# An attention and int8 feed-forward layer on one core: TensorE's order by pairs of slots, and q and k projected into one bank

## The reference

```python
qkv = encodings @ attn_w.T + attn_b                      # 16 heads of 8
mask = jnp.arange(n)[:, None] <= jnp.arange(n)[None, :]
scores = jnp.einsum('bhki,bhqi->bhkq', k, q) / math.sqrt(HEAD)
probs = jax.nn.softmax(jnp.where(mask, scores, NEG_INF), axis=2)
combined = jnp.einsum('bhkq,bhkl->bhql', probs, v)
attn = combined.transpose(0, 2, 1, 3).reshape(b, n, HIDDEN) @ out_w.T + out_b
x = _layernorm(x + attn)
q_lhs = round(x / lhs_scale); q_rhs = round(rhs / rhs_scale)  # int8, absmax scales
x = _layernorm(x + (q_lhs @ q_rhs) * lhs_scale * rhs_scale)
```

## Time and profile before

| | |
|---|---|
| three runs | 284.0, 283.8, 280.09 us; median 283.8 |
| profiled execution | 284.06 us, span 282.3 us, mean granted clock 0.952 |
| PE busy | 244.5 us (87%) |
| DVE busy | 195.1 us (69%) |
| ACT busy | 188.1 us (67%) |
| POOL busy | 121.8 us (43%) |

### The profile page before, as it was taken

One profiled execution on the slowest core, in us unless ns is written; L12 is line 12 of the kernel. 1 busy time (PEld: TensorE's weight loads), 2 busy tenths in 40 slices (PEclk: granted clock), 3 DMA queues, 4 the chain that ended last, 5 costly groups with the idle time before them and its releaser, 6 DMA issues.

```text
span 282.3 us, 8298 instructions
## 1 busy us (share of the span) xinstructions
PE 244.5 (87%) x3075; PEld 171.2 (61%) x3077; DVE 195.1 (69%) x545; ACT 188.1 (67%) x434; POOL 121.8 (43%) x236
## 2 busy tenths in 40 slices
PE   4179747999999999999999999999999999999420
PEld 2037525676767676767676767676767677565200
DVE  7927853576869696868686868686868797624331
ACT  4202033677687787878787878787878777798341
POOL 7930840041525454545453535353535141532542
PEclk9999985999999999999999999999999999999855
DMA  3385777337554765476547654757466410110001
GB/s 93 111 189 121 165 154 196 77 116 152 173 93 134 133 193 92 151 134 192 91 153 135 192 91 151 135 170 118 151 116 190 76 41 15 31 37 16 7 19 37
DMA packets 50887, 32.77 MB, mean 116 GB/s; under 512 B 7200, under 2 KB 50848, under 8 KB 50848
## 3 DMA queue, kind: packets, MB, share of 16 engines
q1 hardware_dynamic: 50848, 32.26, 47.2%
HBM read 17.17 MB, written 14.68 MB: 113 GB/s over the span
## 4 chain that ended last, share of the span: by engine, by line
PE 81%; DVE 7%; issue 4%; POOL 3%; ACT 3%; DMA 1%; ACTq 0%; SPq 0%; POOLq 0%; DVEq 0%
PE pv_bank L860 18%; PE dve_bank L823 17%; PE act_bank L823 13%; PE act_bank L881 6%; PE dve_bank L826 5%; PE act_bank L826 5%; PE act_bank L891 3%; PE dve_bank L905 3%; PE dve_bank L923 3%; PE pv_bank L960 3%; PE act_bank L914 1%; PE dve_bank L871 1%; PE dve_bank L942 1%; PE act_bank L933 1%; POOL rstd L444 1%
## 5 line engine op out<-in xcount | busy, mean ns | idle before, releaser
L642 DVE TRANSPOSE_TENSOR_REDUCE part_max<-dve_bank 128x16 f32<-128x512 f32 (+1 forms) x192 | 115.8, 615 | 42.7 <-PE dve_bank L826 40.6
L481 ACT ACTIVATE probs<-act_bank 128x512 f32<-128x512 f32 (+1 forms) x192 | 101.2, 530 | 38.0 <-PE act_bank L826 37.1
L823 PE MATMUL act_bank<-q_move,k_stat 128*128 128x128 bf16 (+3 forms) x512 | 68.2, 236 | 6.2 <-issue 6.2
L823 PE MATMUL dve_bank<-q_move,k_stat 124*128 124x128 bf16 (+3 forms) x512 | 71.1, 241 | 1.6 <-DMA k_stat<-imagek 1.3
L860 PE MATMUL pv_bank<-probs,v_stat 128*32 128x256 f32 (+3 forms) x1024 | 61.1, 311 | 0.0
L823 PEld LDWEIGHTS dve_bank<-q_move,k_stat 124*128 124x128 bf16 x512 | 40.3, 117 | 28.9 <-DVE part_max L642 7.5
L419 POOL TENSOR_TENSOR qk_rest<-qk_f,qk_parts 128x512 f32<-128x512 f32 x15 | 17.4, 1162 | 75.5 <-ACT qk_f L499 72.4
L823 PEld LDWEIGHTS act_bank<-q_move,k_stat 128*128 128x128 bf16 x512 | 42.0, 114 | 10.7 <-issue 8.2
L826 PE MATMUL dve_bank<-causal,identb 128*128 128x128 bf16 (+1 forms) x192 | 46.5, 242 | 0.0
L826 PE MATMUL act_bank<-causal,identb 128*128 128x128 bf16 (+1 forms) x192 | 46.0, 240 | 0.0
L498 ACT ACTIVATE qk_parts<-act_bank,bias 128x256 bf16<-128x256 f32 x32 | 21.0, 655 | 26.6 <-PE act_bank L881 24.6
(11 more groups left out here) (87 smaller groups left out, 319.1 us busy)
## 6 DMA issues: line engine op xcount, KB each, us to landing
imageq<-qk_parts SPq DMA_DIRECT2D x32, 192.0 KB, 2.1
imagek<-qk_parts SPq DMA_DIRECT2D x32, 192.0 KB, 2.1
q_move<-imageq SPq DMA_DIRECT2D x32, 192.0 KB, 3.7
k_stat<-imagek SPq DMA_DIRECT2D x32, 192.0 KB, 4.4
xt_in<-xt_dram SPq DMA_DIRECT2D x16, 128.0 KB, 4.6
x_in<-x_dram SPq DMA_DIRECT2D x16, 128.0 KB, 2.4
out_dram<-o SPq DMA_DIRECT2D x16, 128.0 KB, 2.0
q_move<-shift SPq DMA_DIRECT2D x32, 8.0 KB
```

The lines of the kernel that those rows point to most:

```text
L481: act.activation(probs[u][:, 0:cols], act_bank[at % ACT_BANKS][:, 0:cols], ACT.Exp, scale=SCALE).then_inc(act_emptied, 1)
L642: dve.tensor_reduce(o32, dve_bank[at % DVE_BANKS][:, 0:n * (TOK - key)].rearrange("k (c q) -> k c q", q=32), op=ALU.max, axis=AX.X, apply_ ...
L823: pe.matmul(tiles[:, j, :], keys, q_move[b % QK_RING][0:rows, p0 + j, key:TOK], start=(j == 0), stop=False, skip_group_check=True)
```

## The change

It replaces the order within a phase. The score units stay where they are, but the other work of TensorE goes only behind odd slots, so that four score units (two for the maximum, two for the exponential) stand together. The value groups are six pairs of units where they were eight groups. q and k of a batch go into the two halves of one `act_bank`; ACT still empties q behind one slot's exponential and k behind the next one's, and only k's last activation says that the bank is empty. Because ACT then empties uses in another order than they were filled, two more tables (`ACT_DONE`, `ACT_FREE`) say what TensorE has to wait for. ACT and DVE have their extras moved to fit: `pv_from_psum` from slot 3 to 4, `norm1` to 5, q to 7 and k to 8, `heads_d` to 9, `round_z` to 10, `norm2` behind the last `zq`; on DVE `scale_ffn` to 3, the shift and both steps of `normalise` to 5.

```diff
-PV_GROUPS = [(0, 1), (2, 3), (4,), (5,), (6, 7), (8, 9), (10,), (11,)]
+PV_GROUPS = [(u, u + 1) for u in range(0, NU, 2)]
...
-ACT_EXTRAS = {1: [("v", 1)], 6: [("q", 4)], 7: [("k", 4)], 8: [("heads", -1)], 11: [("zq", -2)]}
-DVE_EXTRAS = {2: [("ffn", -3)], 4: [("shift", 1)], 5: [("pv", -1)], 11: [("out", -1)]}
+ACT_EXTRAS = {1: [("v", 1)], 7: [("qk", 4)], 9: [("heads", -1)], 11: [("zq", -2)]}
+ACT_EMPTIED = {1: [("v", 1)], 8: [("qk", 4)], 9: [("heads", -1)], 11: [("zq", -2)]}
+DVE_EXTRAS = {3: [("ffn", -3)], 5: [("shift", 1), ("pv", -1)], 11: [("out", -1)]}
...
+ACT_DONE = ring_places(lambda b, u: ("exp", b, u), ACT_EMPTIED)
+ACT_FREE = [max(ACT_DONE[name] for name in list(ACT_AT)[:n + 1]) for n in range(len(ACT_AT))]
...
@@ qk_from_psum
-                act.wait_ge(act_filled, at + 1)
-                src = act_bank[at % ACT_BANKS][:, 0:TOK]
+                    act.wait_ge(act_filled, at + 1)
+                src = act_bank[at % ACT_BANKS][:, w * TOK:(w + 1) * TOK]
...
-                act.activation(whole, src, ACT.Identity, bias=bias[:, w:w + 1]).then_inc(act_emptied, 1)
+                last = act.activation(whole, src, ACT.Identity, bias=bias[:, w:w + 1])
+                if w == 1:
+                    last.then_inc(act_emptied, 1)
...
@@ ScalarE's phase
-                    if u == 3:
+                    if u == 4:
                         pv_from_psum(b - 1)
...
@@ act_ring
-                    pe.wait_ge(act_emptied, at + 1 - ACT_BANKS)
+                    pe.wait_ge(act_emptied, ACT_FREE[at - ACT_BANKS] + 1)
...
@@ project_qk
+                for w in range(2):
+                    last = pe.matmul(bank[:, w * TOK:(w + 1) * TOK], wqkv[:, w, :], xt_in[b % XT_RING][:, :],
+                                     start=(w == 0), stop=True, skip_group_check=True)
+                last.then_inc(act_filled, 1)
...
@@ TensorE's phase, as it is after
+                    if u == 1:
+                        pv(b - 1, 4)
+                        project_v(b + 1)
+                    if u == 3:
                         pv(b - 1, 5)
                         feed_forward(b - 3)
+                    if u == 5:
                         turn_maxima(b + 1)
                         turn_pv(b - 1)
                         pv(b, 0)
+                    if u == 7:
                         pv(b, 1)
+                        project_qk(b + 4)
+                    if u == 9:
                         pv(b, 2)
                         turn_heads(b - 1)
+                    if u == 11:
                         pv(b, 3)
                         project_out(b - 1)
                         turn_zq(b - 2)
```

More of the change, by code:

```diff
@@ L487, in qk_from_psum @@
                     return
-                at = ACT_AT["qk"[w], b]
+                at = ACT_AT["qk", b]
                 if w == 0:
@@ L764, in phase @@
                         join_maxima(b + 1)
-                    if u == 2:
+                    if u == 3:
                         scale_ffn(b - 3)
-                    if u == 4:
+                    if u == 5:
                         make_shift(b + 1, 0)
-                        second_stats(b - 3, 0)
+                        normalise(b - 1, 0)
                         make_shift(b + 1, 1)
-                        second_stats(b - 3, 1)
                         make_shift(b + 1, 2)
-                    if u == 5:
-                        normalise(b - 1, 0)
-                        scales(b - 2, 0)
                         normalise(b - 1, 1)
                     if u == 6:
+                        scales(b - 2, 0)
+                        second_stats(b - 3, 0)
+                    if u == 7:
                         scales(b - 2, 1)
-                    if u == 7:
+                        second_stats(b - 3, 1)
+                    if u == 8:
                         scales(b - 2, 2)
@@ L852, in pv @@
                     wait(pe, pv_out, b - 1)
-                    wait_place(pe, act_emptied, ACT_AT, ("v", b))
-                wait_place(pe, act_emptied, ACT_AT, ("exp", b, us[-1]))
+                    wait_place(pe, act_emptied, ACT_DONE, ("v", b))
+                wait_place(pe, act_emptied, ACT_DONE, ("exp", b, us[-1]))
                 for u in us:
@@ L873, in turn_maxima, with project_qk @@
                 last.then_inc(dve_filled, 1)
-            def project_qk(b, w):
+            def project_qk(b):
                 if not real(b):
                     return
-                if w == 0:
-                    wait_ring(pe, xt_loaded, b, 1)
-                bank = act_ring(("qk"[w], b))
-                pe.matmul(bank[:, 0:TOK], wqkv[:, w, :], xt_in[b % XT_RING][:, :],
-                          start=True, stop=True).then_inc(act_filled, 1)
+                wait_ring(pe, xt_loaded, b, 1)
+                bank = act_ring(("qk", b))
+                for w in range(2):
+                    last = pe.matmul(bank[:, w * TOK:(w + 1) * TOK], wqkv[:, w, :], xt_in[b % XT_RING][:, :],
+                                     start=(w == 0), stop=True, skip_group_check=True)
+                last.then_inc(act_filled, 1)
             def project_v(b):
@@ L919, in project_out @@
                     return
-                wait_place(pe, act_emptied, ACT_AT, ("heads", b))
+                wait_place(pe, act_emptied, ACT_DONE, ("heads", b))
                 bank = dve_ring(("out", b))
@@ L938, in feed_forward @@
                     return
-                wait_place(pe, act_emptied, ACT_AT, ("zq", b))
+                wait_place(pe, act_emptied, ACT_DONE, ("zq", b))
                 bank = dve_ring(("ffn", b))
```

37 lines of the change are left out of this document (10 added, 27 removed).

## The result

The changed kernel takes 289.73 us (median of 4 runs, 287.92 to 290.35), the kernel before 283.86 beside it: a ratio of 1.023, 95% interval 1.013 to 1.033. Its profiled execution took 290.09 us, with a span of 288.4. It is slower, by 6 us and not by the 10 forecast.

A forecast was written before the change was run, and what follows sets the result against it. TensorE, busy for nearly all of each 14.14 us batch, was the bound. Phases 1 to 11 +7.9, phase 0 +0.1, phases 12 and 13 +0.2 each, end +0.3, head +1.7: +10.4 on 284.06 gives 294.5 us, range 285.5 to 299.

The forecast's parts named there:

- TensorE's own work: TensorE's work per batch without the new waits: from 14.14 us down to 13.56.
- Wait A: TensorE waits at the turn of the value sums for ACT's copy of `pv_bank`: 0.60 us a batch (0.45 to 0.65).
- Wait B: TensorE waits ahead of unit 10's scores for the bank of q and k: 0.70 us a batch (0.55 to 0.75).
- the 0.11: k's projection behind a value group: first weight load exposed by the change of tile, 0.11 us, covered right behind q.
- small waits: Around the turn of the maxima and slot 5: waits for DVE that go, 0.15 us a batch (0 to 0.15).
- Period: Time between turns of the value sums of neighbouring batches: 14.86 us up to phase 11.
- What is late next: DVE's q and k cast and slot 11's maxima: bank free 5.5 us after slot 8 starts, wanted at 5.6; just fits.
- Rival 3: A further wait, at the cast or a DVE bank, 0.2 to 0.4 us a batch: 297 to 300 us; chance 0.09.
- Head: Before the batches flow: first q +0.8 us, q of batch 2 +0.9, together +1.7 (0 to 2).
- The last two and the tail, thinner on PE, +0.3: End of the launch, where TensorE has less work: 0.3 us longer.
- one wait only: One of the two ScalarE waits does not bite: 286.1 us without either one; chance 0.14.
- none: ACT's releases are off TensorE's path, so neither wait bites: 13.56 us a batch, 278.0 us; chance 0.09.

The follow-up runs named there:

- experiment 7: Kernel before with only the value groups of units 4 and 5, and of 10 and 11, joined: 276.32 us, ratio 0.978.
- Experiment 1: Changed kernel with ScalarE's copy of the value sums put back behind unit 3's exponential: 280.53 us, ratio 0.991 to the kernel before.
- experiment 4: Kernel before with only the copy of the value sums moved from behind unit 3's exponential to behind unit 4's: 290.77 us, ratio 1.027.
- Experiment 6: Kernel before with q and k projected into one bank and both emptied in slot 7: 290.02 us, ratio 1.025.
- experiment 2: Changed kernel with both halves of the q and k bank emptied in slot 7: 285.02 us, ratio 1.007 to the kernel before.
- experiment 9: Kernel before with the changed kernel's VectorE order behind the turn of the value sums: 280.66 us, ratio 0.992.
- experiment 10: Changed kernel with VectorE's second statistics put back ahead of the heads' normalisation: 290.77 us, ratio 1.029 to the kernel before.
- experiment 3: Changed kernel with the copy back behind unit 3's exponential and q and k both emptied in slot 7: 277.15 us, ratio 0.980 to the kernel before.

## Why the prediction was right, and where it was not

**TensorE's own work: right in sum, by parts that made up for each other.** 14.79 less A (0.50 to 0.54) less B (0.67) is 13.58 to 13.62; the sum said 13.56. The joins gave 0.46 for 0.40: the merged group of 128 and 64 columns takes 0.47 (143.33 to 143.80) where the two took 0.35 and 0.25, and a way in is gone, twice over. q and k together take 0.97 (141.27 to 142.24), which is the 0.54 and 0.43 of the text; but experiment 7 shows that of the 0.11 only 0.05 belongs to the change of tile, the rest goes where k stands right behind q. The output projection behind values pays 0.10 (146.46 to 147.01, 0.55, where it took 0.45), for the 0.08 taken. The turn of the heads behind values pays 0.05, which the sum left out (143.80 to 144.07, 0.27; 152.67 to 152.89, 0.22, in before). The 0.15 of small waits was misread: the turn of the maxima takes 0.34 in experiments 1 and 7 too, so no wait for DVE was in it. From unit 4's last product through slot 5 and the maxima it is 1.01 now (0.67 from 151.68 to 152.35, and 0.34) for 1.10: 0.09.

**Wait A: right**, 0.50 to 0.54 for 0.60. The chain from unit 4's last product to the turn was 1.51 (151.68 to 153.19) for 1.55: the way from ACT to PE took 0.06 (153.13 to 153.19), not the 0.13 that I had put in as an estimate. PE's side took 1.01 for 0.95. Experiment 1 takes the wait out of after (0.54), experiment 4 puts it into before (0.44).

**Wait B: right**, 0.67 for 0.70; the bank came free 2.73 after the start of slot 8 (142.24 to 144.97), for 2.78. That is 0.28 + 0.73 + 0.37 + 0.57 + 0.73 + 0.05 by the starts of the rows, where the text had 0.20, 0.72, 0.43, 0.58, 0.73 and 0.12; no run shows the 0.12. Experiment 6 shows that one bank for q and k is enough for such a wait, experiment 2 that emptying in two steps lengthens the period by 0.31.

**Period: right**, 14.79 for 14.86; over the eleven periods from phase 1 to 12 the turns are 162.47 us apart where they were 155.02: +7.4, for +7.9.

**What is late next: it just fits**, as the text had it. DVE's timeline of after:

```profile
146.75 0.43 DVE L661 CAST qk_parts<-qk_rest 128x512 bf16<-128x512 f32 x1 [1.67 <-POOL qk_parts L425]
147.09 0.57 DVE L647 TRANSPOSE_TENSOR_REDUCE part_max<-dve_bank 128x12 f32<-128x384 f32 x1
```

The cast starts 1.83 after k is done (144.92), DVE stands idle 1.67 for it, and the maxima behind it still empty the bank in time: the next phase's 64-column scores for the maximum start at 147.84 with no wait. Rival 3 did not come.

**Head: +1.7 forecast, +1.3 seen, and not settled.** DVE's first step on q and k starts at 8.13 for 7.21, +0.9 for +0.8; that repeats in all profiles (7.2 to 7.5 with two banks, 7.9 to 8.1 with one). The exponentials start at 45.63 for 44.29, where 46.0 was forecast. But kernels with the same head differ here: 42.9 to 44.4 in eight with two banks, 43.9 to 45.6 in six with one. Their means are 1.0 apart, less than either spread. The granted clock from that start to 60 us differs too, 0.81 to 0.90 over the fourteen. No experiment isolated the second half of this term.

**The tail is the step that failed.** "The last two and the tail, thinner on PE, +0.3": from the last turn to the end it took 21.0 us before and 18.2 after, **-2.8**. I had costed the moves on DVE at nothing, since in the steady part DVE has room; there they cost nothing (period 14.14 in experiment 9). At the end no next batch covers DVE's queue, and the reciprocal stood behind 2.18 us of waiting for GpSimd. The moves that mattered, the scale of z and the second statistics behind `normalise`, are not even in the list of moves ahead of the prediction. Experiment 9 shows -2.0 of the tail by DVE's order, and experiment 10 gives 2.4 back by one part of it. The other 0.8 is ScalarE's `norm2` behind the last copy of z, read from the traces under experiment 9; that move is in the list, and I gave it no price. The spans add up: +1.2 to the first turn, +7.4, +0.3 to the last turn (+0.4 forecast and a part of the tail's 0.3), -2.8: +6.1. With -2.8 for +0.3 the forecast would have been 291.4, against 290.09 for the profiled execution; most of the rest is the head and A and B, each a little smaller than forecast.

**The rivals.** Neither "one wait only" nor "none" came; experiments 1 and 3 are these cases: 280.5 and, with half of B left, 277.2. I had given 286.1 and 278.0 for them. The period of experiment 1 is as given (14.25 for 14.26); the two ends are not: the tails are 17.6 and 17.7 where the forecast left them near 21, and the first turns stand at 63.63 and 62.83 where it had 65.2. The clock stayed at 1.00, the 2.4 GHz level, in every steady window, after as before. Two waits of 0.5 to 0.7 us in each 14.8 did not lower it, and so what "TensorE: Matmul & The Clock Gate" of the Trainium skill, section A second HAM failure mode, warns of (short idles from cycling banks) is not borne out by this kernel.

## What to carry to other kernels

Price a regrouping by its parts: here the joins gained 0.46 us a batch, and two waits cost 1.2. One came by the place of a single line. The other came with q and k in one bank, which saved 0.11 and made PE wait 0.67, 0.31 of it even when both are emptied at once. When a hand-written queue is rearranged, write down for every consumer on the bounding engine what now stands ahead of its producer, and put a producer ahead of work that would leave its engine idle anyway. Cost moves on a non-bounding engine in the tail as well, where an in-order queue that waits for someone else delays the chain that ends the kernel.

## What was not expected of the hardware

- Going from the whole array to tiles of 32 columns and back costs TensorE some 0.2 us each time, over and over: a value group joined to another gives 0.23 (0.10 on the way in, 0.13 for the way out and the restart), and five bursts fewer give 1.17. 1.17 us is 8% of a batch, in a kernel whose TensorE looked full.
- ACT's q and k activations on the same 128 x 256 values print 0.85 and 0.73 us where they write four strips of 64 with a step of four elements (k), and 0.47 each where they write in order (q). From the first's start to the second's end that is 1.30 for 0.84. It was in the sum, by rows, but it makes k the expensive half of a shared bank.
- The start of the exponentials, behind a chain of four engines and HBM, moves by some 1.5 us between kernels whose head is the same. A difference of 1 us in the whole time of single profiles can come from there.
